# Two attentions of a Flamingo layer pair: heads written out without a loop, new orders of TensorE's work within a step, and identity matmuls

## The chip, the core and the metric

The kernel runs on one core of a Trainium2 chip. The metric is the device time in microseconds (us) of one execution; before the change the median of three runs is 1977.64 us (1966.12 to 1983.28). The core has five engines that run beside each other and meet at semaphores: TensorE (matmuls; PE in the profile, its weight loads PEld), VectorE (DVE), ScalarE (ACT), GpSimd (POOL) and SyncE (SP), which here issues transfers.

## The reference

Two layers, each a gated cross-attention and a gated mixture of experts, over 2048 tokens of width 256 and 1601 context rows:

```python
x = x + jnp.tanh(g_xattn[0]) * _L0_xattn_ref(_layernorm(x), ctx, ctx, mask, ...)
x = x + jnp.tanh(g_ffn[0])   * _L0_ffn_ref(_layernorm(x), ...)
x = x + jnp.tanh(g_xattn[1]) * _L1_xattn_ref(_layernorm(x), ctx, ...)
x = x + jnp.tanh(g_ffn[1])   * _L1_ffn_ref(_layernorm(x), ...)
```

Both attentions have 16 heads of depth 16:

```python
q, k, v = _proj(query, wq, bq), _proj(ctx, wk, bk), _proj(ctx, wv, bv)
scores = jnp.einsum('bhqd,bhkd->bhqk', q, k) / 4
scores = jnp.where(mask == 0, -jnp.inf, scores)     # layer 0 only
x = jnp.einsum('bhqk,bhkd->bhqd', jax.nn.softmax(scores, axis=-1), v)
return jnp.einsum('bsd,ed->bse', x, wo) + bo
```

In layer 0 the mask leaves nearly all keys out: the mask is zero for the keys that are valid. The kernel finds the keys that count at run time, and where they fit into a window of 512 keys it attends to that window alone. They do for these inputs. Layer 1 attends to all 1601 keys.

## The kernel before

`flamingo_kernel` runs stages one after the other: projections of the context, normalisation and queries, `attend_masked` (layer 0), output projection, experts, and the same for layer 1 with `attend`. The change touches `attend` (L589 on) alone, which both attentions use, with a `Keys` object for the sizes: the windowed one has KT = 4 key tiles of 128 and one maxima piece of 512 keys for each query tile; the full one has KT = 13 and four pieces of 399 to 402 keys. A third branch, all keys with the mask, isn't taken.

For each head three kinds of work are done, and three heads are in flight at once. **Maxima**: queries times keys with the queries as weights, in pieces of a PSUM bank, of which VectorE takes the row maxima (L793, L900); 64 pieces a head in the full attention, 16 in the windowed one. TensorE then turns the finished maxima (L782), VectorE splits them into two parts (L906, L908), and SP sends these as two more rows of the queries (L726). **Scores**: keys times queries, with the maxima subtracted by those rows, in four chunks of 512 queries for each key tile (L804); ScalarE takes the exponential of each (L883). **Values**: probabilities times values for the four chunks of a key tile, in four column groups of the array, accumulated in one bank over the head (L821); column 16 of the values is one and so gives the sums. ScalarE copies the bank out (L866), TensorE turns it with four transposes (L786, "sums"), VectorE divides (L916, L919).

Queries and keys lie twice in SBUF, once on partitions 0 to 50 and once on 64 to 114; 48 to 51 rows are contracted, so a matmul takes one half of the array's rows. Score chunks 0 and 2 use the lower half, 1 and 3 the upper; maxima pieces take turns (`tile_of`, piece number modulo 2). Scores have three banks (`s_bank`), pieces, turned maxima and sums share four (`p_bank`), values have one.

An iteration `i` has KT steps. It makes the maxima of head i, all but the last LATE key tiles' scores of head i-1 (from step LATE on), and the last LATE key tiles of head i-2 (steps 0 to LATE-1); values follow one step behind their scores. LATE is 4 in the full and 2 in the windowed attention. `entries` lists the pieces of each step (four or five; four in the windowed one), with "maxima" put in at step 1 (windowed: step 0) behind two pieces, and "sums" last in step 6 (windowed: 3). `body` of the tensor block (L826 on) writes out the order of a step by hand: chunks 0 and 1, two pieces, chunk 2, one piece, values, chunk 3, the rest. Waits: a score waits until the exponential three chunks before has freed its bank; a piece waits until VectorE has done the piece four places before; the first score of a head waits for the two rows with its maxima; a head's first values wait until the bank has been copied out. ScalarE's copy stands in step LATE before chunk 3's exponential.

`iterations` (L681 on) gives the order of heads to each engine: iterations 0 to 3 written out, 4 to 15 as a loop of four passes over three iterations, 16 and 17 written out. SP has a loop of its own of the same form.

## Time and profile before

| | us |
|---|---|
| three runs | 1966.12, 1977.64, 1983.28 |
| the profiled execution | 1979.84 |
| its span, first to last instruction | 1978.0 |
| TensorE busy | 1660.8 (84%) |
| VectorE busy | 1051.4 (53%) |
| ScalarE busy | 767.8 (39%) |
| maxima pieces on VectorE (L900), 1280 | 672.6 |
| exponentials on ScalarE (L883), 1088 | 565.5 |
| maxima matmuls on TensorE (L793), 1280 | 425.8 |
| score matmuls on TensorE (L804), 1088 | 410.5 |
| values matmuls on TensorE (L821), 2176 records | 325.4 |
| mean granted clock of TensorE | 0.873 |

The busy times of an engine's lines are unions and can overlap with each other. The two attentions lie at about 169 to 408 us (windowed) and 995 to 1670 us (full) of the span.
### The profile page before, as it was taken

The page shows a single profiled execution, that of the slowest core. Times are in us where ns is not written, and L with a number is a line of the kernel's source. Part 1 is how long each engine was busy: PE and PEld are TensorE (multiplying, and loading weights), DVE is VectorE, ACT ScalarE, POOL GpSimd, SP SyncE. Part 2 cuts the span into 40 slices and gives each one's busy share as a digit, 9 for nine tenths or more (in the row PEclk, how much of TensorE's full clock was granted, in tenths as well). Part 3 has the DMA queues.
Part 4 walks back from the last instruction along what each step waited for, and adds up shares of the span by engine and source line. Part 5 has one row for each costly group of instructions (what it writes and reads, how often), then busy time and mean ns, then how long its engine had stood idle before and what let it go on. Part 6 is the DMA issues. An engine that isn't in the chain of part 4 may idle for free. (4 is left out here: it accounts for less than half of the span.)

```text
span 1978.0 us, 26775 instructions
## 1 busy us (share of the span) xinstructions
PE 1660.8 (84%) x7489; PEld 864.0 (44%) x7490; DVE 1051.4 (53%) x2222; ACT 767.8 (39%) x1486; POOL 174.5 (9%) x243
## 2 busy tenths in 40 slices
PE   6465999969998999994499999999999999786880
PEld 3132444345665566662254444444444433543550
DVE  2565688652211122224398888787887841522334
ACT  3031577621111121120317776676776774121110
POOL 3610000000300000003000000000000000051106
PEclk9785699978999999997759998898998995697995
DMA  7934221111100987882632121111211100424114
GB/s 245 365 139 130 56 49 49 26 44 64 43 0 22 328 304 286 305 304 80 181 86 64 41 42 22 24 22 24 42 22 23 23 2 0 106 77 130 40 45 130
DMA packets 108696, 197.16 MB, mean 100 GB/s; under 512 B 8958, under 2 KB 80371, under 8 KB 108567
## 3 DMA queue, kind: packets, MB, share of 16 engines
q1 hardware_dynamic: 101633, 180.71, 29.3%
q0 software_dynamic: 4608, 12.59, 2.0%
q10 hardware_dynamic: 2326, 2.31, 0.4%
q8 instruction: 61, 1.00, 0.2%
q14 instruction: 68, 0.56, 0.1%
HBM read 144.69 MB, written 50.36 MB: 99 GB/s over the span
## 5 line engine op out<-in xcount | busy, mean ns | idle before, releaser
L900 DVE TENSOR_REDUCE attend_piece_max<-attend_p_bank 128x1 f32<-128x400 f32 (+3 forms) x1280 | 672.6, 590 | 155.3 <-PE attend_p_bank L793 147.5
L883 ACT ACTIVATE attend_probs<-attend_s_bank 128x512 f32<-128x512 f32 (+1 forms) x1088 | 565.5, 601 | 333.4 <-PE attend_s_bank L804 332.8
L793 PE MATMUL attend_p_bank<-attend_k_st,attend_q_st 48*128 48x400 f32 (+2 forms) x1280 | 425.8, 432 | 47.0 <-DMA attend_k_st<-ones_rows 21.1
L804 PE MATMUL attend_s_bank<-attend_q_st,attend_k_st 50*128 50x512 f32 (+2 forms) x1088 | 410.5, 493 | 32.7 <-ACT attend_probs L883 11.8
L804 PEld LDWEIGHTS attend_s_bank<-attend_q_st,attend_k_st 50*128 50x128 f32 (+2 forms) x1088 | 182.2, 198 | 385.5 <-ACT attend_probs L883 307.3
L821 PE MATMUL attend_o_bank<-attend_probs,attend_v_st 128*32 128x512 f32 (+1 forms) x2176 | 325.4, 673 | 1.4 <-ACT attend_probs L883 1.4
L793 PEld LDWEIGHTS attend_p_bank<-attend_k_st,attend_q_st 48*128 48x128 f32 (+1 forms) x1280 | 231.7, 207 | 92.4 <-issue 43.9
L1498 DVE TENSOR_TENSOR slots_hid<-slots_b_bank,slots_g_act 128x512 f32<-128x512 f32 x46 | 31.8, 692 | 159.9 <-PE slots_b_bank L1392 159.9
L1279 DVE TENSOR_TENSOR share_hid<-share_b_bank,share_g_act 128x512 f32<-128x512 f32 (+1 forms) x40 | 27.6, 691 | 149.1 <-PE share_b_bank L1160 149.1
L1468 ACT ACTIVATE slots_g_act<-slots_a_bank 128x512 f32<-128x512 f32 x46 | 27.5, 597 | 169.4 <-PE slots_a_bank L1392 169.4
L1392 PE MATMUL slots_a_bank<-slots_w_up,slots_x_t 128*128 128x512 f32 x184 | 88.1, 602 | 5.4 <-DMA slots_w_up<-in_L_ffn_W_dram 5.4
L1392 PE MATMUL slots_b_bank<-slots_w_up,slots_x_t 128*128 128x512 f32 x184 | 86.5, 592 | 0.0
L1414 PE MATMUL slots_y_bank<-slots_w_dn,slots_hid_t 128*128 128x256 f32 x368 | 83.3, 379 | 1.0 <-DVE slots_hid_t L1455 1.0
L1707 POOL DMA_INDIRECT collect_back<-back,keep_f_place x48 | 46.7, 974 | 422.6 <-PEq L1696 408.6
L1414 PEld LDWEIGHTS slots_y_bank<-slots_w_dn,slots_hid_t 128*128 128x128 f32 x368 | 69.8, 190 | 20.0 <-issue 11.7
L1160 PE MATMUL share_a_bank<-keep_x_x_nt,share_w_up 128*128 128x512 f32 (+1 forms) x160 | 78.6, 615 | 0.0
L1610 PE MATMUL slots_u_bank<-keep_f_up,slots_x_t 128*128 x156 | 63.6, 532 | 17.8 <-issue 15.9
L821 PEld LDWEIGHTS attend_o_bank<-attend_probs,attend_v_st 128*32 128x32 f32 (+1 forms) x2176 | 44.5, 112 | 76.9 <-ACT attend_probs L883 57.0
L1131 POOL DMA_INDIRECT sorted<-keep_x_x_n,keep_f_place x48 | 46.4, 966 | 349.3 <-DVE keep_f_place L1264 335.3
L768 POOL COPY attend_v_st<-attend_values 128x64 f32 (+3 forms) x32 | 9.3, 298 | 768.7 <-PE attend_o_bank L821 737.0
L1160 PE MATMUL share_b_bank<-keep_x_x_nt,share_w_up 128*128 128x512 f32 (+1 forms) x160 | 76.3, 600 | 0.0
L1171 PE MATMUL share_y_bank<-share_w_dn,share_hid 128*128 128x256 f32 (+1 forms) x320 | 71.2, 382 | 5.9 <-DVE share_hid L1279 5.9
(208 smaller groups left out, 1368.2 us busy)
## 6 DMA issues: line engine op xcount, KB each, us to landing
slots_w_up<-in_L_ffn_W_dram SPq DMA_DIRECT2D x46, 1024.0 KB, 6.9
slots_w_dn<-in_L_ffn_W_dram SPq DMA_DIRECT2D x23, 1024.0 KB, 6.7
ctx_raw<-in_mask_BxSxS_ik_dram SPq DMA_DIRECT2D x16, 800.5 KB, 8.3
q_rows<-q_part SPq DMA_DIRECT2D x24, 512.0 KB, 4.0
attend_q_st<-q_rows SPq DMA_DIRECT2D x64, 192.0 KB, 4.5
k_rows<-ctx_k_part SPq DMA_DIRECT2D x12, 800.5 KB, 10.5
attend_k_st<-k_rows SPq DMA_DIRECT2D x32, 300.2 KB, 5.9
sorted<-keep_zeros SPq DMA_DIRECT2D x6, 1024.0 KB, 6.7
```

The source lines that it names most:

```text
L793: last = pe.matmul(bank[:, 0:even(kn)], q_st[rows, slot, t * P:(t + 1) * P].bitcast(F32R), k_st[rows, slot, k0:k0 + even(kn)].bitcast(F32R ...
L804: last = pe.matmul(out, k_st[rows, hs, kt * P:kt * P + kn].bitcast(F32R), q_st[rows, hs, q0:q0 + CH].bitcast(F32R), start=True, stop=not m ...
L821: last = pe.matmul(o_bank[c * VW:(c + 1) * VW, :], v_st[0:kn, hs, kt, :], probs[0:kn, (kt + hs) % RING, c * CH:(c + 1) * CH], start=(kt == ...
L883: act.activation(probs[0:kn, (kt + hs) % RING, q0:q0 + CH], s_bank[(NC * kt + c + hs) % RING][0:kn, :], ACT.Exp).then_inc(exp_done, 1)
L900: dve.tensor_reduce(dst, bank_of(i, n)[:, 0:kn], AX.X, ALU.max).then_inc(entry_done, 1)
L1131: pool.indirect_dma_start(scratch["sorted"][l][:, :], bass.IndirectOffsetOnAxis(ap=place[:, k, t:t + 1], axis=0), x_n[:, t], None).then_in ...
L1160: last = pe.matmul(bank[n % 2][0:FW, :], w_up[:, which, b, f * FW:(f + 1) * FW], x_nt[:, b, c * CH:(c + 1) * CH], start=(b == 0), stop=(b ...
L1171: last = pe.matmul(y_bank[n % 2][:, :], hid[:, c % 2, f, t * P:(t + 1) * P], w_dn[:, f], start=(f == 0), stop=(f == FT - 1))
L1392: last = pe.matmul(bank[k][:, 0:HW], x_t[:, slot, b], w_up[:, slot, which, b, half * HW:(half + 1) * HW], start=(b == 0), stop=(b == DB - 1))
L1414: last = pe.matmul(y_bank[:, 0:D], hid_t[:, slot, f], w_dn[:, slot, f], start=(f == 0), stop=(f == FT - 1))
L1610: last = pe.matmul(u_bank[k][:, 0:2 * F], x_t[:, k, b], resident["up"][:, e, b].rearrange("p a n f -> p (a n f)"), start=(b == 0), stop=(b ...
L1707: pool.indirect_dma_start(back[:, k, t], None, scratch["back"][l][:, :], bass.IndirectOffsetOnAxis(ap=place[:, k, t:t + 1], axis=0))\
```

## The change

`Keys` gets a flag `looped`; only the branch that isn't taken sets it, so for both attentions that run, every engine's iterations and SP's are written out. In `body` of the tensor block a step has one of two orders, by the half of its first piece (EVEN: lower, also where a step has no pieces; ODD: upper), and values come after all scores and pieces, followed by the sums. `keep_busy` multiplies a bf16 identity by itself, four times repeated to 512 columns, into the bank that the next entry will overwrite: twice ahead of the turned maxima and of the sums, twice ahead of each piece in steps 0 and 1 of the windowed attention's iteration 1, and twelve times in iteration 16 ahead of the wait for the last head's maxima. ScalarE's copy of the values' bank moves from step LATE before chunk 3 to step LATE+1 before chunk 2.

```diff
--- before.py
+++ after.py
@@ -380,7 +380,8 @@
 class Keys:
 
 
-    def __init__(self, first, size, pieces, late, maxima_at):
+    def __init__(self, first, size, pieces, late, maxima_at, looped=False):
+        self.looped = looped
         self.first, self.S, self.pieces = first, size, pieces
         self.KT = -(-size // P)
         self.late = late
@@ -637,6 +638,11 @@
         ENTRIES = PER + 4
         assert ENTRIES % BANKS == 0 and (NC * KT) % RING == 1
 
+        EVEN = [("entry", slice(0, 2)), ("score", 0), ("score", 1), ("entry", slice(2, 4)), ("score", 2), ("score", 3),
+                ("entry", slice(4, None))]
+        ODD = [("entry", slice(0, 1)), ("score", 0), ("score", 1), ("entry", slice(1, 2)), ("entry", slice(2, 3)),
+               ("score", 2), ("entry", slice(3, 4)), ("score", 3), ("entry", slice(4, None))]
+
         def entries(mx, tail, fresh):
 
 
@@ -682,11 +688,12 @@
 
             def once(i):
                 body(i, i % RING, i < H, i >= 2, 1 <= i <= H)
-            for i in range(4):
+            for i in range(4 if keys.looped else H):
                 once(i)
-            with eng.Fori(4, H - RING + 1, RING) as j:
-                for u in range(RING):
-                    body(j + u, (4 + u) % RING, True, True, True)
+            if keys.looped:
+                with eng.Fori(4, H - RING + 1, RING) as j:
+                    for u in range(RING):
+                        body(j + u, (4 + u) % RING, True, True, True)
             for i in range(H, H + 2):
                 once(i)
 
@@ -744,10 +751,11 @@
                 for t, n in clears[2 * i - 2:2 * i]:
                     sp.dma_start(scratch["sorted"][l][t * P:(t + n) * P, :].rearrange("(t p) d -> p t d", p=P),
                                  const["zeros"][:, :].unsqueeze(1).to_broadcast([P, n, D])).then_inc(cleared, 16)
-            with sp.Fori(4, H - RING, RING) as j:
-                for u in range(RING):
-                    body(j + u, (4 + u) % RING, True, True, True)
-            for i in range(H - RING, H + 1):
+            if keys.looped:
+                with sp.Fori(4, H - RING, RING) as j:
+                    for u in range(RING):
+                        body(j + u, (4 + u) % RING, True, True, True)
+            for i in range(H - RING if keys.looped else 4, H + 1):
                 body(i, i % RING, True, True, True)
             sp.wait_ge(cleared, 16 * len(clears))
 
@@ -774,9 +782,16 @@
             pe.wait_ge(fixed, 2 + (SP > S))
             pe.wait_ge(rows_in, 16 * (6 if row_masked else 2))
 
-            def entry(i, slot, what, n):
+            def keep_busy(bank, times):
+
+                for _ in range(times):
+                    pe.matmul(bank[:, :], const["ident_bf"][:, :],
+                              const["ident_bf"][:, :].unsqueeze(1).to_broadcast([P, CH // P, P]), start=True, stop=True)
+
+            def entry(i, slot, what, n, extra=0):
                 wait(pe, entry_done, entries_before(i) + (n - BANKS + 1))
                 bank = bank_of(i, n)
+                keep_busy(bank, extra if extra else 2 * isinstance(what, str))
                 if what == "maxima":
                     wait(pe, max_ready, i)
                     last = pe.transpose(bank[0:QT, 0:P], row_max[:, (slot - 1) % RING, :], const["ident"][:, :])
@@ -833,14 +848,24 @@
                 for s in range(KT):
                     now, before = score_step(i, slot, s, tail, fresh), pv_step(i, slot, s, tail, fresh)
                     if now and now[2] == 0:
+                        if isinstance(i, int) and i == H:
+                            pe.wait_ge(entry_done, entries_before(i) + places("maxima"))
+                            keep_busy(p_bank[0], 12)
                         wait(pe, max_in, i * (16 * PART))
-                    for chunks, first, end in (((0, 1), 0, 2), ((2,), 2, 3), ((3,), 3, None)):
-                        if chunks == (3,) and before:
-                            times_values(*before)
-                        for c in chunks if now else ():
-                            scores(*now, c)
-                        for what, at in listed[s][first:end]:
-                            entry(i, slot, what, at)
+                    raising = row_masked and isinstance(i, int) and i == 1 and s < LATE
+                    pieces = [x for x in listed[s] if x[0] != "sums"]
+                    sides = [what % 2 for what, _ in pieces if not isinstance(what, str)]
+                    order = ODD if sides and sides[0] else EVEN
+                    for kind, at in order:
+                        if kind == "score" and now:
+                            scores(*now, at)
+                        elif kind == "entry":
+                            for what, n in pieces[at]:
+                                entry(i, slot, what, n, 2 * raising)
+                    if before:
+                        times_values(*before)
+                    for what, n in listed[s][len(pieces):]:
+                        entry(i, slot, what, n)
 
             iterations(pe, body)
 
@@ -868,7 +893,7 @@
             def body(i, slot, mx, tail, fresh):
                 for s in range(KT):
                     now = score_step(i, slot, s, tail, fresh)
-                    if not now and s == LATE and tail:
+                    if not now and s == LATE + 1 and tail:
                         copy_out(i)
                     if now:
                         h, hs, kt = now
@@ -876,7 +901,7 @@
                         if not isinstance(h, int) or KT * h + kt >= RING:
                             wait(act, pv_done, h * KT + (kt - 2))
                         for c in range(NC):
-                            if c == NC - 1 and s == LATE and tail:
+                            if c == 2 and s == LATE + 1 and tail:
                                 copy_out(i)
                             q0 = chunk_of(c)
                             wait(act, score_ready, h * (NC * KT) + (NC * kt + c + 1))
@@ -1765,7 +1790,8 @@
         }
         x_now, stats = sc.sb("x_now", [P, QT, D], F32), sc.sb("stats", [P, QT, 6], F32)
         make_constants(nc, io, const, scratch)
-        everything = Keys(0, S, PIECES, 4, (1, 2))
+        everything = Keys(0, S, PIECES, 4, (1, 2), looped=True)
+        unmasked = Keys(0, S, PIECES, 4, (1, 2))
         for l in range(2):
             if l:
                 clear_semaphores(nc)
@@ -1788,7 +1814,7 @@
                 if l == 0:
                     attend_masked(nc, const, scratch, everything, attn, row_max, mask_all, window)
                 else:
-                    attend(nc, const, scratch, l, everything, attn, row_max)
+                    attend(nc, const, scratch, l, unmasked, attn, row_max)
                 project_out(nc, const, l, attn, row_max, io["x"][0] if l == 0 else None, x_now, stats)
             with ExitStack() as part:
                 keep = Scope(nc, part, f"keep_f{l}")
```

## Rows read from the trace of the kernel before

**Rows 1.** Windows, the two attentions: busy us (instructions) of each engine, clock, DMA

```profile
177.60:242.70 65.10, 63.89 (x243) 27.38 (x243) 44.23 (x82) 31.53 (x61) 0.71 (x3) 0.58 0.30 84
242.70:380.70 138.00, 131.47 (x756) 55.50 (x756) 122.54 (x232) 97.39 (x188) 2.37 (x10) 1.00 0.18 44
1168.00:1211.70 43.70, 42.69 (x226) 18.56 (x225) 33.50 (x70) 27.44 (x54) 0.36 (x1) 0.80 0.13 25
1211.70:1249.00 37.30, 35.04 (x220) 15.10 (x219) 33.25 (x69) 26.83 (x52) 0.36 (x1) 1.00 0.17 29
1249.00:1292.80 43.80, 40.45 (x231) 18.22 (x231) 33.39 (x69) 28.11 (x55) 0.36 (x1) 0.88 0.14 26
1367.50:1412.20 44.70, 41.87 (x231) 18.91 (x231) 33.42 (x70) 28.27 (x55) 0.36 (x1) 0.85 0.13 25
1486.90:1533.60 46.70, 43.34 (x231) 19.62 (x231) 33.42 (x70) 28.27 (x55) 0.36 (x1) 0.82 0.13 24
```

**Rows 2.** Timeline at a pass of the loop: start, length, instructions, idle before

```profile
1251.12 0.91 PE L804 MATMUL attend_s_bank<-attend_q_st,attend_k_st 50*128 50x512 f32 x2 [3.08 <-issue]
```

**Rows 3.** Waits, full attention: who waited for whom, us in total, times, longest

```profile
PEld attend_s_bank L804 <- ACT attend_probs L883: 239.0, 366, 1.7
```

**Rows 4.** Timeline of TensorE, two regular steps of the full attention

```profile
1156.49 0.49 PE L804 MATMUL attend_s_bank<-attend_q_st,attend_k_st 50*128 50x512 f32 x1
1156.83 0.34 PE L793 MATMUL attend_p_bank<-attend_k_st,attend_q_st 48*128 48x400 f32 x1
1157.10 1.06 PE L821 MATMUL attend_o_bank<-attend_probs,attend_v_st 128*32 128x512 f32 x8
1158.09 0.49 PE L804 MATMUL attend_s_bank<-attend_q_st,attend_k_st 50*128 50x512 f32 x1
...
1158.39 0.39 PE L804 MATMUL attend_s_bank<-attend_q_st,attend_k_st 50*128 50x512 f32 x1
...
1158.61 0.39 PE L804 MATMUL attend_s_bank<-attend_q_st,attend_k_st 50*128 50x512 f32 x1
1158.62 0.56 PE L793 MATMUL attend_p_bank<-attend_k_st,attend_q_st 48*128 48x400 f32 x2
1159.28 0.50 PE L804 MATMUL attend_s_bank<-attend_q_st,attend_k_st 50*128 50x512 f32 x1
1159.43 0.44 PE L793 MATMUL attend_p_bank<-attend_k_st,attend_q_st 48*128 48x400 f32 x1
1159.81 0.64 PE L821 MATMUL attend_o_bank<-attend_probs,attend_v_st 128*32 128x512 f32 x4
```

**Rows 5.** Timeline of TensorE, steps without maxima pieces, tail of the full attention

```profile
1626.07 0.49 PE L804 MATMUL attend_s_bank<-attend_q_st,attend_k_st 50*128 50x512 f32 x1 [0.45 <-ACT attend_probs L883]
1626.49 1.06 PE L821 MATMUL attend_o_bank<-attend_probs,attend_v_st 128*32 128x512 f32 x8
...
1629.13 1.93 PE L821 MATMUL attend_o_bank<-attend_probs,attend_v_st 128*32 128x512 f32 x8
...
1633.20 1.08 PE L821 MATMUL attend_o_bank<-attend_probs,attend_v_st 128*32 128x512 f32 x4
```

**Rows 6.** Page, costliest groups: the exponentials, busy us, mean ns, idle before

```profile
L883 ACT ACTIVATE attend_probs<-attend_s_bank 128x512 f32<-128x512 f32 (+1 forms) x1088 | 565.5, 601 | 333.4 <-PE attend_s_bank L804 332.8
```

**Rows 7.** Page, costliest groups: 512-column f32 matmuls over the full array

```profile
L1392 PE MATMUL slots_a_bank<-slots_w_up,slots_x_t 128*128 128x512 f32 x184 | 88.1, 602 | 5.4 <-DMA slots_w_up<-in_L_ffn_W_dram 5.4
```

**Rows 8.** Timeline of TensorE, full head, around the sums

```profile
1228.76 1.06 PE L821 MATMUL attend_o_bank<-attend_probs,attend_v_st 128*32 128x512 f32 x8
...
1230.36 0.66 PE L786 MATMUL attend_p_bank<-keep_ident,attend_o_sb 128*128 128x128 f32 x4
1230.95 0.50 PE L804 MATMUL attend_s_bank<-attend_q_st,attend_k_st 50*128 50x512 f32 x2
...
1232.23 0.44 PE L793 MATMUL attend_p_bank<-attend_k_st,attend_q_st 48*128 48x400 f32 x1 [0.22 <-DVE keep_a_attn L919]
1232.60 0.64 PE L821 MATMUL attend_o_bank<-attend_probs,attend_v_st 128*32 128x512 f32 x4
```

## The prediction

> **What bounds the kernel now.** I read the stages first, by windows over each head of the two attentions, then the granted clock in them, then what TensorE waits for, then TensorE's own timeline. The first attention is the windowed one (four key tiles), the second the full one (thirteen). A full head at the upper clock (2.4 GHz, granted 1.00) takes 37.3 us [rows 1]: thirteen steps, in which TensorE is busy 35.0 us, VectorE 33.3 and ScalarE 26.8. Neither VectorE nor ScalarE is full. Three heads, the first of each later pass of the loop, take 43.8, 44.7 and 46.7 us [rows 1], and there TensorE stands still 3.08 us for "issue", with nothing that it waits for, before its first score chunk [rows 2]; then the granted clock falls to 0.50 (1.2 GHz) for part of the head, which makes the mean 0.82 to 0.88. One head, 1168.0 to 1211.7, is as slow (43.7 us, clock 0.80) with no such gap. The other cold places are the windowed attention's first heads (177.6 to 242.7, clock 0.58) and the tails, where only scores and values are left: there a step is 2.64 us long (1626.49 to 1629.13) and then, at the lower clock, 4.07 [rows 5].
>
> Inside a step at the upper clock the longest wait is the weight load of a score chunk for the exponential that frees its bank: 239.0 us in the full attention [rows 3]. The timeline shows the ring [rows 4]. With the values starting at 1157.10, the next work starts at 1158.09 (+0.99): score chunk 3. The next score starts at 1158.39 (+1.29), behind a piece in its half. Chunk 2 of the next key tile starts at 1159.28, 1.19 after chunk 3, since its bank is freed by chunk 3's exponential (three banks, four chunks). A piece follows, and the values start at 1159.81. So 0.99 + 1.19 + 0.53 = 2.71 us per step; where the piece after chunk 2 shares its half (1156.49, 1156.83, 1157.10) the last term is 0.61 and the step 2.79; with no piece it is 0.42 (1626.07 to 1626.49) [rows 5]. Mean of both kinds 2.75. That ring, not the columns that TensorE streams, sets the step.
>
> **The change, part by part.**
>
> *No loop.* The three gaps and the cold stretches behind them cost 43.8 + 44.7 + 46.7 - 3 x 37.3 = 23.3 us, and the same instructions in a straight line leave no such gap in the heads before the loop. I take -23. Bounds: -9 (the gaps alone, 3 x 3.1, if the clock falls anyway) to -30 (the unprovoked fall, 6.4 us, goes too). The windowed attention's eleven heads from 242.7 to 380.7 take 12.5 us each with clock 1.00 [rows 1], so its loop costs nothing that can be won. SP's and POOL's bodies are unrolled too; their loads stay behind the same waits, a head ahead.
>
> *The orders in a regular step.* The ring keeps its form: values, first score, its exponential, the score three chunks later, values. It is now chunk 0 that comes first and chunk 3 that waits for it. In an even step (first piece in half 0) two pieces stand ahead, chunk 0 is second in its half: its start moves from +0.99 to +1.29, but a score that starts first has its weight load in front (0.49 against 0.39 long), so its result is late by 0.30 - 0.10 = 0.20 [rows 4]. Chunk 3 then starts at 2.38, the fifth piece is in the other half: 2.38 + 0.53 = 2.91. In an odd step the one piece ahead is in the other half, chunk 0 starts at +0.99, the fifth piece shares chunk 3's half: 2.18 + 0.61 = 2.79. Step 0 has four pieces: 2.38 + 0.42 = 2.80. So the new orders do not shorten a regular step; they lengthen even ones by 0.1 to 0.2. The pieces add nothing: VectorE is busy 33.3 of 37.3 us [rows 1], a step's five pieces take it some 2.5 us of these 2.8 to 2.9, and its four banks carry it over the values' 0.99; if it were late, the wait of the fifth piece for the bank of the first would be next.
>
> *Copy out of the values' bank.* It moves one step on and behind two exponentials. The next values wait for it: first exponential at about 1.73, two at 0.52 (565.5 us over 1088), the copy, of the same shape, 0.60 [rows 6]: values at 3.3 instead of 2.91, against about 2.95 in the old order (chunk 2 held by 0.2): +0.35. Formerly it went ahead of chunk 3's exponential and held chunk 2 a little. Queued behind it on ScalarE are chunks 2 and 3, ready in time.
>
> *Identity matmuls.* Two ahead of each transpose of the maxima and of the sums, 512 columns of bf16, full array. No row has one. Bounds: 0 if they fall wholly in a wait, 0.47 each from 512-column f32 records (88.1 us over 184) [rows 7]. I take 0.23, the distance at which the next work in the same half follows a 512-column score (1158.39 to 1158.62; nearest in columns and in being one record) [rows 4]. Sums: formerly the first transpose starts at 1230.36 and scores resume at 1230.95, values at 1232.60, 3.84 after those of 1228.76 [rows 8], because the third maxima piece (1232.23) waits until the sums are normalised, 1.87 after the first transpose; some 0.4 of these VectorE spends on a piece queued before. Now: values 0, identities 1.0, transposes 1.65, resumed at 2.2, chunk 0 at 2.5, chunk 3 at 3.55, the fifth piece needs VectorE (sums normalised at 3.15, first piece done at 3.7): values at 4.1. Maxima: formerly they came last before the values, where only the values' own change of mode followed. Now they stand between chunk 1 and the third piece: two more changes between half and full array; the last piece waits for the split maxima, about 3.15: values at 3.5.
>
> Full head: 2.80 + 3.5 + 6 x 2.79 + 3 x 2.91 + 3.3 + 4.1 = 39.2 against 37.3: +1.9, times 14 heads: **+26**. Bounds: -57 if every step shrank to VectorE's 33.3 us per head; +40 with identities at 0.47.
>
> *Windowed head.* Four even steps of four pieces. The two regular ones tie (chunk 0 later by 0.2, but no piece between chunk 3 and the values, 0.42 against 0.61). The copy costs +0.4; sums and maxima now follow each other with four identities and the second waits for the normalised sums: +1.1. +1.5 x 14 = **+21**. Bounds: 0 and +34.
>
> *Raising the clock.* In iteration 1 of the windowed attention two identities stand ahead of each of eight pieces (16 at twice 0.23 while cold, 7 us, partly over the wait for the first maxima). From 177.6 to 242.7 four iterations take 65.1 us [rows 1]; at 12.5 us each, with some 2.5 for identities that nothing covers, they would take 52.5. So -13 if the clock rises there and stays. Bounds: +4 (it doesn't rise) to -15.
>
> *Twelve at the end*, before head 15's first score in both attentions: 12 x 0.23 + 0.1 = 2.9 us each on the path, as nothing is queued that could hide them. A tail step costs 1.43 more at 1.2 GHz [rows 5]. If they hold the clock for four more steps in the windowed tail and three in the full one, they return 10: -4 net. Bounds: +6 to -15.
>
> **Sum**: -23 + 26 + 21 - 13 - 4 = +7 on the profiled execution's 1979.8 us, which lies 2.2 over the median 1977.6: **1984 us**.
>
> **A rule weighed.** In the rows a weight load is hidden even in the same half: the piece at 1158.62 follows its score by 0.23 us, no more than 512 columns' stream at 2.4 GHz. The Trainium skill (TensorE: Matmul & The Clock Gate, Part 3, "What overlaps and what doesn't") says that a weight load overlaps a running matmul only when the row group differs. By that rule opposite halves side by side would save a load on one or two neighbours a step. The trace disagrees wherever the load is not behind a semaphore; behind one it shows 0.61 against 0.53, a gain of 0.08. A second one speaks against the change: TensorEngine Tiling (Array Packing), "Key Properties", has a change of tiling mode drain the array; the added switches at the maxima would be dearer than I take them.
>
> **Rivals.**
> 1. *The orders cost nothing* (27%). If the identities and the copy lie in waits that the ring has anyway (239 us of them), the 26 and 21 vanish: 1984 - 47 = 1937. For it: TensorE waits about 1.1 us a step for ScalarE. Against: those waits lie ahead of the third-next score, and the additions stand ahead of the first.
> 2. *Same-half neighbours were the price* (6%): behind a wait, a piece starts 0.34 after a score of its own half and 0.15 after one of the other (1156.83, 1159.43) [rows 4]; 0.19 saved in each of 208 + 64 steps is 52 us: 1984 - 52 = 1932. The skill's rule above would give this.
> 3. *The clock falls more often* (20%), the other side. Regular steps stretch, so TensorE does less per us; the head from 1168.0, slow without a gap, shows how near the level is [rows 1]. Place: the copy and sums steps of full heads. Each fall costs 6.4. Three more, and no rise in the windowed attention (+17): 1984 + 19 + 17 = 2020. It decides from two further falls (1997).
> 4. *The identities do hold the clock* (4%): no unprovoked fall, windowed and full tails warm: 1984 - 6 - 20 = 1958.
> 5. My forecast, 43%, own range 1962 to 2006; of it 6% lies above +1%.
>
> A change under 1% (20 us) is what a measurement of this kernel cannot tell from none: its three runs span 17 us. Faster by over 1%: 27 + 6 + 4 = 37%. Slower: 20 + 6 = 26%. Within: 37%. The range takes rivals 1 and 2 in with room for partly hidden terms (1925) and stops between my upper bound and rival 3 (2012).
>
> **What would show it.** No "issue" gap of 3 us at heads 7, 10 and 13; full heads of 39 us where the clock is 1.00 (rival 1: 37.3; rival 2: below 35); first score at +1.29 in even steps and +0.99 in odd ones, values to values 2.9 and 2.8; about 4.1 after the sums. Windowed heads of 14 us; clock 1.00 from about 190 us. Wrong it would be, above all, if chunk 3 didn't wait for chunk 0's exponential, or if the cold stretches stay though the gaps go.

## The result and the profile after

The changed kernel takes 2033.16 us (median of four, 2029.45 to 2037.07) against 1977.18: the ratio is 1.029, 95% interval 1.0239 to 1.0341. It is slower by 2.9%, above the range. A ratio here and below compares only those executions of a kernel whose clock was little disturbed, and so can say more or less than the medians. The page of the profiled execution (2029.45 us); PEclk is the granted clock in 40 slices, in tenths:

```profile
span 2027.7 us, 23161 instructions
...
PE 1680.6 (83%) x7657; PEld 848.2 (42%) x7658; DVE 1052.9 (52%) x2222; ACT 767.0 (38%) x1486; POOL 173.6 (9%) x243
...
PEclk9785999988999999996669899898999995797995
```

TensorE is busy longer, at about the same mean clock, and the tenths drop to 8 again and again over the full attention. Windows over the two attentions (busy us and instructions of PE, PEld, DVE, ACT, POOL; clock; DMA) answer to [rows 1]; the last row is the full attention's tail:

```profile
178.60:241.10 62.50, 57.64 (x273) 21.23 (x273) 44.67 (x83) 31.05 (x60) 0.71 (x3) 0.83 0.31 88
241.10:395.60 154.50, 136.16 (x801) 52.86 (x801) 122.69 (x231) 97.30 (x187) 2.38 (x10) 1.00 0.16 40
1155.00:1197.20 42.20, 38.75 (x231) 15.96 (x231) 33.27 (x69) 27.44 (x53) 0.36 (x1) 0.92 0.14 25
1240.30:1279.60 39.30, 35.93 (x231) 14.95 (x233) 33.28 (x70) 27.43 (x53) 0.36 (x1) 1.00 0.16 27
1651.30:1719.70 68.40, 61.28 (x234) 16.76 (x235) 1.46 (x5) 35.70 (x70) 0.00 (x0) 0.65 0.00 1
```

The windowed attention's eleven later heads take 154.5 / 11 = 14.05 us each, formerly 12.5. A full head at the upper clock takes 39.3 us, formerly 37.3, with VectorE busy the same 33.3. But such heads are rare: of the fifteen intervals between the ends of heads' maxima in the full attention, nine are 42 to 43 us like the one from 1155.0, clock 0.92, and one is 40.5. A head's maxima count as ended when VectorE begins to join them. Summed over the profiles, from the first head's maxima to the last's, the full attention went from 590.9 to 619.9 us (+29.0), the windowed one from 203.1 to 217.0 (+13.9), the tails behind them from 24.6 to 25.0 and from 58.5 to 68.4 (+10.3); the rest gives 3.5 back; the span's difference is 49.7.

Two regular steps answer to [rows 4]:

```profile
1187.54 1.07 PE L836 MATMUL attend_o_bank<-attend_probs,attend_v_st 128*32 128x512 f32 x8
1188.54 0.44 PE L808 MATMUL attend_p_bank<-attend_k_st,attend_q_st 48*128 48x402 f32 x1
1188.54 0.67 PE L819 MATMUL attend_s_bank<-attend_q_st,attend_k_st 50*128 50x512 f32 x2
...
1189.78 0.50 PE L819 MATMUL attend_s_bank<-attend_q_st,attend_k_st 50*128 50x512 f32 x1
1190.12 0.34 PE L808 MATMUL attend_p_bank<-attend_k_st,attend_q_st 48*128 48x400 f32 x1
1190.39 1.07 PE L836 MATMUL attend_o_bank<-attend_probs,attend_v_st 128*32 128x512 f32 x8
1191.39 0.45 PE L808 MATMUL attend_p_bank<-attend_k_st,attend_q_st 48*128 48x400 f32 x2
1191.68 0.40 PE L819 MATMUL attend_s_bank<-attend_q_st,attend_k_st 50*128 50x512 f32 x2
...
1192.82 0.49 PE L819 MATMUL attend_s_bank<-attend_q_st,attend_k_st 50*128 50x512 f32 x1 [0.32 <-ACT attend_probs L908]
...
1193.24 0.64 PE L836 MATMUL attend_o_bank<-attend_probs,attend_v_st 128*32 128x512 f32 x4
```

The ring has the form that was foretold. In the odd step a piece and the first score start together at 1188.54 (+1.00), chunk 3 at 1189.78 (+2.24), then a piece of its own half, and the values at 1190.39: 2.85 in all. In the even step two pieces start (1191.39), the scores follow behind them (+1.29), chunk 3 starts at 1192.82 (+2.43) together with its piece, and the values at 1193.24: again 2.85. The waits, which answer to [rows 3], have moved from scores behind exponentials to pieces behind VectorE, without anything gained. The first row is the kernel before, beside the 239.0 us of [rows 3]; the other two are the changed kernel:

```profile
PEld attend_p_bank L793 <- DVE attend_piece_max L900: 13.9, 54, 0.5
PEld attend_p_bank L808 <- DVE attend_piece_max L925: 126.6, 171, 1.7
PEld attend_s_bank L819 <- ACT attend_probs L908: 101.8, 176, 1.1
```

The step with the copy of the values' bank, TensorE's rows and then ScalarE's:

```profile
1168.97 1.07 PE L836 MATMUL attend_o_bank<-attend_probs,attend_v_st 65*32 65x512 f32 x8
...
1171.39 0.50 PE L819 MATMUL attend_s_bank<-attend_q_st,attend_k_st 50*128 50x512 f32 x1 [0.33 <-ACT attend_probs L908]
...
1172.41 1.59 PE L836 MATMUL attend_o_bank<-attend_probs,attend_v_st 128*32 128x512 f32 x8 [0.53 <-issue]
1173.93 0.70 PE L808 MATMUL attend_p_bank<-attend_k_st,attend_q_st 48*128 48x400 f32 x1
```

```profile
1170.74 1.09 ACT L908 ACTIVATE attend_probs<-attend_s_bank 128x512 f32<-128x512 f32 x2 [0.97 <-PE attend_s_bank L819]
1171.71 0.60 ACT L891 ACTIVATE attend_o_sb<-attend_o_bank 128x512 f32<-128x512 f32 x1
1172.19 1.10 ACT L908 ACTIVATE attend_probs<-attend_s_bank 128x512 f32<-128x512 f32 x2
```

The last score starts at 1171.39, its piece with it; the values could follow at 1171.8 (estimated from the 0.42 us between them in the even step). But the copy (L891) starts only at 1171.71, behind two exponentials, and TensorE stands, that is, has nothing to do, for 0.53 us; the step is 1172.41 - 1168.97 = 3.44 us. What follows at 1173.93 starts 1.52 behind the values instead of 1.0: the granted clock falls to 0.50 at 1172.8. In each of the ten slow heads the clock falls in this step: copies that start at 1086.4, 1128.4, 1171.7, 1213.7, 1296.1, 1339.1, 1381.1, 1463.5, 1506.5 and 1625.8 us, and falls recorded at 1087.5, 1128.5, 1172.8, 1213.8, 1295.7, 1340.1, 1381.0, 1463.0, 1507.3 and 1626.8. In the kernel before, the two falls that no loop's return explains lay at the same place, 1.2 and 1.9 us behind the start of a copy (falls at 1181.8 and 1509.5).

The stand isn't always ahead of the fall, though. Five of the ten falls are recorded 0.9 to 1.1 us behind the start of the copy, two as it starts, and three (1295.7, 1381.0, 1463.0) before it. At the last of these the score ahead of the stand is already long, 0.79 us instead of 0.50:

```profile
1463.15 0.79 PE L819 MATMUL attend_s_bank<-attend_q_st,attend_k_st 50*128 50x512 f32 x1 [0.33 <-ACT attend_probs L908]
...
1464.18 1.94 PE L836 MATMUL attend_o_bank<-attend_probs,attend_v_st 128*32 128x512 f32 x8 [0.23 <-issue]
```

So the stand of the same step can't have brought down the clock in these three; that stands are the cause at all has to be shown by taking them away.

### The profile page after: what moved, and what is told of

It reads as the page before. It is cut to its first block and busy times, and to the rows that moved or that the text cites. A ratio compares the mean times of both kernels' runs of the same rounds, so it can differ in the third digit from the quotient of the medians.

```text
span 2027.7 us, 23161 instructions
## 1 busy us (share of the span) xinstructions
PE 1680.6 (83%) x7657; PEld 848.2 (42%) x7658; DVE 1052.9 (52%) x2222; ACT 767.0 (38%) x1486; POOL 173.6 (9%) x243
## 5 line engine op out<-in xcount | busy, mean ns | idle before, releaser
L808 PE MATMUL attend_p_bank<-attend_k_st,attend_q_st 48*128 48x400 f32 (+2 forms) x1280 | 388.6, 445 | 46.5 <-DMA attend_k_st<-ones_rows 20.9
L819 PE MATMUL attend_s_bank<-attend_q_st,attend_k_st 50*128 50x512 f32 (+2 forms) x1088 | 374.9, 461 | 57.4 <-ACT attend_probs L908 49.4
L836 PE MATMUL attend_o_bank<-attend_probs,attend_v_st 128*32 128x512 f32 (+1 forms) x2176 | 319.5, 662 | 15.1 <-issue 15.1
L808 PEld LDWEIGHTS attend_p_bank<-attend_k_st,attend_q_st 48*128 48x128 f32 (+1 forms) x1280 | 196.6, 203 | 302.1 <-DVE attend_piece_max L925 178.7
L819 PEld LDWEIGHTS attend_s_bank<-attend_q_st,attend_k_st 50*128 50x128 f32 (+2 forms) x1088 | 166.1, 196 | 184.7 <-ACT attend_probs L908 162.5
L941 DVE RECIPROCAL attend_inv_sum<-attend_p_bank 128x16 f32<-128x16 f32 x32 | 8.2, 257 | 143.3 <-PE attend_p_bank L801 143.3
L776 POOL COPY attend_v_st<-attend_values 128x64 f32<-128x64 f32 (+1 forms) x32 | 9.4, 300 | 804.9 <-PE attend_o_bank L836 774.5
```

What stands on the lines that cost most here:

```text
L808: last = pe.matmul(bank[:, 0:even(kn)], q_st[rows, slot, t * P:(t + 1) * P].bitcast(F32R), k_st[rows, slot, k0:k0 + even(kn)].bitcast(F32R ...
L819: last = pe.matmul(out, k_st[rows, hs, kt * P:kt * P + kn].bitcast(F32R), q_st[rows, hs, q0:q0 + CH].bitcast(F32R), start=True, stop=not m ...
L836: last = pe.matmul(o_bank[c * VW:(c + 1) * VW, :], v_st[0:kn, hs, kt, :], probs[0:kn, (kt + hs) % RING, c * CH:(c + 1) * CH], start=(kt == ...
```

## The experiments

All were timed beside the kernel before. Medians of that kernel moved between 1970 and 1979 us from one group to the next. Names that begin with a stand for edits of the changed kernel, those with b for edits of the kernel before. "Copy step" is the time from values to values, in the full attention and at 2.4 GHz, in the step in which ScalarE copies the values' bank out. "Falls" counts falls of the clock between the first and the last head's maxima of the full attention in one execution, the profiled one, and such counts differ between executions: the profiled one of `b_noloop_late` was the fastest of its four, those of `a_nobusy` and `b_noloop_later` the slowest and second slowest.

| kernel | median us | ratio (95%) | copy step | full, windowed head at 2.4 GHz | falls |
|---|---|---|---|---|---|
| before | 1970 to 1979 | 1 | 2.97 | 37.3, 12.5 | 5 |
| after | 2033 | 1.029 (1.024 to 1.034) | 3.45 | 39.3, 14.0 | 10 |
| b_noloop | 1941.6 | 0.980 (0.972 to 0.988) | 2.88 | 37.1, 12.3 | 2 |
| b_noloop_late | 1937.5 | 0.989 (0.977 to 1.001) | 3.20 | 37.5, 12.6 | 0 |
| b_noloop_later | 2007.7 | 1.010 (1.000 to 1.020) | 3.70 | 37.9, 13.1 | 7 |
| b_noloop_raise | 1936.7 | 0.987 (0.978 to 0.997) | 2.88 | 37.1, 12.3 | 3 |
| b_sooner | 1925.2 | 0.976 (0.971 to 0.981) | 2.78 | 37.7, 11.8 | 1 |
| b_sooner_raise | 1926.2 | 0.976 (0.971 to 0.981) | 2.78 | 37.7, 11.8 | 0 |
| b_mixed | 1936.6 | 0.977 (0.969 to 0.986) | 2.89 | 37.1, 11.8 | 3 |
| b_one | 1955.4 | 0.991 (0.987 to 0.995) | 2.80 | 38.3, 11.8 | 5 |
| a_looped | 2074.6 | 1.047 (1.039 to 1.055) | 3.39 | 38.8, 14.0 | 11 |
| a_nobusy | 2026.4 | 1.021 (1.013 to 1.029) | 3.45 | 38.9, 13.7 | 12 |
| a_no12 | 2023.8 | 1.026 (1.016 to 1.036) | 3.45 | 39.3, 14.0 | 10 |
| a_copy | 1976.7 | 1.009 (1.006 to 1.012) | 2.80 | 38.6, 13.4 | 2 |
| a_copy_nobusy | 1976.5 | 1.001 (0.996 to 1.006) | 2.80 | 38.2, 13.0 | 5 |
| a_copy_first | 1963.4 | 0.997 (0.992 to 1.001) | 2.75 | 38.2, 12.8 | 4 |
| a_late_first | 1986.4 | 1.008 (1.002 to 1.013) | 3.26 | 38.7, 13.3 | 7 |

**The loop.** `b_noloop` writes out the loops of the kernel before, with nothing else (the hunks of the change with `looped` in them). `a_looped` puts them back into the changed kernel:

```diff
-        unmasked = Keys(0, S, PIECES, 4, (1, 2))
+        unmasked = Keys(0, S, PIECES, 4, (1, 2), looped=True)
```

and the same flag for the windowed keys.

> The kernel before with only its loops written out; orders, copy and identities as before. Theory A (the loop's gaps pull the clock down, and the changed kernel lost that gain by its later copy out of the values' bank): full heads of 37.3 us, no issue gap of 3 us, at most two clock falls between heads 2 and 15, time 1977 - 23 = 1954 (1945 to 1962). Theory B (without the loop the clock falls at head boundaries anyway, since the gaps were not the cause): cold heads every second or third one, time 1970 to 1985. Theory C (straight-line code is fetched more slowly): steps longer than 2.71 and 2.79 at the upper clock, over 1985.

> The changed kernel with its loops kept (orders, copy and identities stay). Theory A: the three gaps of 3 us come back at heads 7, 10 and 13 with cold stretches beside the falls at the copy: 2033 + 9 to + 20 = 2042 to 2053. Theory B (the clock falls anyway): only the gaps themselves return, 2042. If writing the loop out gained nothing at all: 2033.

Writing the loops out is worth 37 us by the medians before the change (1941.6) and 41 after it (2074.6 against 2033.2), more than the 23 that I took; the ratios say 39 and 35. `a_looped` came out slower than any of its three expectations. Two falls were left in `b_noloop`; the first of them cost 10 us. In its profile 19 us were gained in the full attention, 3 in the windowed one (heads of 12.3 instead of 12.5 us, so that loop cost something too) and 16 in the tails, whose iterations were written out before as well; these 16 are a later fall of the clock, and no run shows that the loop has a part in them.

**The copy.** `a_copy` takes the copy ahead of chunk 0's exponential in the same step of the changed kernel:

```diff
-                            if c == 2 and s == LATE + 1 and tail:
+                            if c == 0 and s == LATE + 1 and tail:
```

> The changed kernel with ScalarE's copy of the values' bank ahead of chunk 0's exponential in the same step instead of chunk 2's. Theory A: the values no longer stand 0.5 us for the copy, step 5 is 2.9 to 3.0 instead of 3.45, full heads 38.8, windowed 13.5, and the falls at the copy go (at most three in the full attention instead of nine): 2033 - 8 - 8 - 25 = 1992. Theory B or D: the steps shorten the same way but the falls stay: 2015 to 2020.

It measures 1976.7, faster than the 1992 of theory A: by the medians one line gives back the whole of the change's 56 us, by the ratios (1.029 to 1.009) some 40. Its copy step and a stretch of nine heads without a fall:

```profile
1187.37 1.06 PE L836 MATMUL attend_o_bank<-attend_probs,attend_v_st 65*32 65x512 f32 x8
...
1189.74 0.50 PE L819 MATMUL attend_s_bank<-attend_q_st,attend_k_st 50*128 50x512 f32 x1 [0.26 <-ACT attend_probs L908]
...
1190.16 0.64 PE L836 MATMUL attend_o_bank<-attend_probs,attend_v_st 128*32 128x512 f32 x4
```

```profile
1041.60:1383.00 341.40, 316.77 (x2022) 131.31 (x2021) 294.09 (x610) 243.37 (x471) 3.25 (x9) 1.00 0.18 36
```

There is no stand ahead of the values at 1190.16. Of the 56 us, 20 are 0.7 us in each full and 0.65 in each windowed head, 25 are falls in the full attention (its time over 15 heads at the upper clock went from 30.4 to 5.2 us), and 8 lie in the full tail. This doesn't hang on the one profile: worked out from span and mean granted clock (twice the missing share, times the span), the four executions of the changed kernel spent 483 to 507 us each at 1.2 GHz, the ten of `a_copy` 370 to 420. `b_noloop_late` and `b_noloop_later` bring the stand to the old orders, written out and without identities:

```diff
-                            if c == NC - 1 and s == LATE and tail:
+                            if c == 1 and s == LATE + 1 and tail:
```

with `c == 2` in the second, and in both the line for steps without scores one step on, as in the change.

> The kernel before, written out, with ScalarE's copy of the values' bank moved one step on and ahead of chunk 1's exponential, so that the next values wait for it by some 0.4 us; old orders, no identities. Theory A: full heads 37.2 + 0.3 = 37.5 and windowed 12.3 + 0.3, and falls of the clock at the copy in most heads (+3 to 4 each, 14 heads): 1942 + 10 + 40 = 1990. If only the late copy together with the new orders does it: 1952, with three falls or fewer.

> The kernel before, written out, with the copy one step on and ahead of chunk 2's exponential: in the old order the values then stand about 0.9 us for it instead of 0.4. Theory A1: with a stand twice that of the changed kernel the clock falls at every copy, 1940 + 7 + 7 + 45 = 1999. Theory A2: the other steps of the head stay at 2.75, at most three or four falls, 1940 + 14 + 5 = 1959.

With the copy behind one exponential TensorE stands 0.34 us in each head, and in the profiled execution the clock stays at 1.00 from 1022.8 to 1579.2 us, nearly the whole attention:

```profile
1202.31 1.06 PE L824 MATMUL attend_o_bank<-attend_probs,attend_v_st 65*32 65x512 f32 x8
...
1204.83 0.34 PE L796 MATMUL attend_p_bank<-attend_k_st,attend_q_st 48*128 48x400 f32 x1
1205.52 1.07 PE L824 MATMUL attend_o_bank<-attend_probs,attend_v_st 128*32 128x512 f32 x8 [0.34 <-issue]
```

```profile
1022.80:1579.20 556.40, 531.24 (x3327) 231.26 (x3327) 482.94 (x1001) 408.52 (x790) 4.71 (x13) 1.00 0.16 30
```

Behind two it stands 0.84 us, and the clock falls at about every second copy, in six of seven falls for 17 us:

```profile
1157.36 1.06 PE L824 MATMUL attend_o_bank<-attend_probs,attend_v_st 65*32 65x512 f32 x8
...
1161.06 0.64 PE L824 MATMUL attend_o_bank<-attend_probs,attend_v_st 128*32 128x512 f32 x4 [0.84 <-issue]
```

```profile
1134.50:1199.40 64.90, 61.20 (x386) 26.74 (x388) 57.86 (x120) 47.93 (x93) 0.72 (x2) 1.00 0.17 30
1199.40:1216.40 17.00, 17.00 (x70) 7.84 (x62) 8.87 (x19) 6.97 (x15) 0.00 (x0) 0.50 0.07 11
1216.40:1281.30 64.90, 61.24 (x386) 26.79 (x388) 57.86 (x120) 47.81 (x93) 0.72 (x2) 1.00 0.16 30
```

Over all executions `b_noloop_later` spent 490 to 576 us at 1.2 GHz and `b_noloop` 409 to 464; `b_noloop_late`, with 361 to 461, isn't set apart from `b_noloop`. My theory as first written (any such stand) fell with the first of the two; and A2, by which the stretched steps around the stand are needed, fell with the second, whose regular steps are the old 2.71 and 2.79. `a_late_first` (the changed kernel, late copy, chunk 0 first as below) was to part these two:

> The changed kernel (late copy, identities, written out) with chunk 0 ahead of the first two pieces in even steps, so that only the regular steps get shorter (2.85 to 2.72) while the values still stand for the copy. Theory A1 (the stand of the values itself pulls the clock down): still eight or nine falls at the copy, 2033 - 6 - 9 = 2018. Theory A2 (the stand does it only where the steps around it are stretched too, since TensorE then does too little in the whole stretch): three falls or fewer, 2033 - 15 - 25 = 1993.

It lies between: seven falls, but all of one head in two at the copy, and most cost only 1.2 us instead of 3 to 4. So neither order nor stand settles it alone: with the copy step at 3.20 us there was no fall, with 3.26, 3.39, 3.45 and 3.70 there were seven to twelve, in old and new orders, and what each cost depended on the order around it. Nor is a stand needed for every fall: the five of `a_copy_nobusy` and three of the five of `b_one` come 1 to 2 us behind copies that nothing waits for. The clock is apt to fall at this place in all kernels; with the long stand it falls there often. How the stand does that stays open.

**The identities.** `a_nobusy` and `a_copy_nobusy` have none; `a_no12` lacks the twelve of iteration 16; `b_noloop_raise` adds only those of the windowed attention's iteration 1, meant to raise the clock there ("raising" below), to the written-out kernel before.

```diff
-                keep_busy(bank, extra if extra else 2 * isinstance(what, str))
+                keep_busy(bank, extra)
...
-                    raising = row_masked and isinstance(i, int) and i == 1 and s < LATE
+                    raising = False
...
-                            keep_busy(p_bank[0], 12)
```

> The changed kernel without any identity matmul; orders, copy and written-out heads stay. Theory A (late copy holds the values 0.5 us and the clock falls there): the falls stay, one head in two, at the copy; full heads at the upper clock 39.3 - 0.9 = 38.4; windowed heads 14.05 - 0.9 = 13.1, their first ones cold again (+7); time 2033 - 13 - 13 + 7 - 6 = 2008. Theory B (the identities are what tips the clock, by the drains around them): no falls inside the full attention, 1980. Theory D (the identities hold the clock as far as it is held): falls at every head, over 2040.

> The changed kernel with the early copy and without any identity matmul. If the late copy alone pulls the clock down (theory A), no more than three falls in the full attention and full heads at 38.6 - 0.5 = 38.1, windowed 13.0, first windowed heads cold (+7): 1977 - 8 - 6 + 7 = 1970. If the identities also hold the clock (theory D), falls at the sums of most heads (+3 to 4 us each): 2000 or more.

> The changed kernel without the twelve identities ahead of the last head's scores. If they only cost: the step of 5.35 us in the full tail becomes 2.66 and that of the windowed tail loses as much: 2033 - 6 = 2027. If they hold the clock in the tails (returning 10 as the forecast had it): 2033 + 4 = 2037, with cold stretches that begin earlier in both tails.

> The kernel before, written out, with the identities in the windowed attention's iteration 1 alone (two ahead of each of eight pieces and of the maxima). If they raise the clock there: 1.00 from about 200 us, iterations 1 to 4 take 18 + 3 x 12.4 + 2 = 57 us instead of 65, time 1942 - 8 = 1934. If the clock rises no earlier than 233: 1942 + 4 = 1946.

Those at the head boundaries cost 0.4 us a head, where 0.92 are streamed: the step of the sums takes 3.82 us with them and 3.43 without, the step of the maxima 3.54 either way. With them less time was spent at 1.2 GHz (370 to 420 against 411 to 488 us, ten executions each, early copy; in the profiles 10 us of the difference lie ahead of the rise in the windowed attention). The sum is nil (1976.5 against 1976.7). The twelve cost what they take, 2.76 us here:

```profile
1661.36 1.06 PE L836 MATMUL attend_o_bank<-attend_probs,attend_v_st 128*32 128x512 f32 x8
1662.36 2.76 PE L788 MATMUL attend_p_bank<-keep_ident_bf 128*128 128x512 bf16 x12
1665.06 0.73 PE L819 MATMUL attend_s_bank<-attend_q_st,attend_k_st 50*128 50x512 f32 x3
...
1666.72 0.64 PE L836 MATMUL attend_o_bank<-attend_probs,attend_v_st 65*32 65x512 f32 x4
```

They return nothing in the full tail, where the clock fell at 1671.2 all the same; without them the median is 9 us lower, within what the intervals leave open. The raising identities make iteration 1 14.7 to 20.2 us long (18.5 in the changed kernel) instead of 10.3 to 12.5. The clock rose at 183 to 202 us in the eight profiles with them and at 187, 188, 190, 190, 199, 211, 223, 233 and 233 us in the nine without. So they replace a wide spread by a narrower one, at a price of four to eight us; `b_noloop_raise` is no faster than `b_noloop` beyond their intervals, nor `b_sooner_raise` than `b_sooner`.

**The orders.** `a_copy_first` is `a_copy` with chunk 0 ahead of the pieces in even steps (the line's first half):

```diff
-        EVEN = [("entry", slice(0, 2)), ("score", 0), ("score", 1),
+        EVEN = [("score", 0), ("entry", slice(0, 2)), ("score", 1),
```

> The changed kernel with the early copy, and in even steps chunk 0 ahead of the first two pieces. Ring theory (the first score after the values, its exponential, the score three later): even steps go from 2.85 to 2.7 (0.99 + 1.19 + 0.53), odd ones stay at 2.8; full heads 38.6 - 7 x 0.14 = 37.7, windowed 13.4 - 4 x 0.17 = 12.7, time 1977 - 13 - 10 = 1954. If the pieces in front cost nothing (VectorE or the streams set the step): 1977.

```profile
1198.31 1.06 PE L836 MATMUL attend_o_bank<-attend_probs,attend_v_st 128*32 128x512 f32 x8
1199.30 0.49 PE L819 MATMUL attend_s_bank<-attend_q_st,attend_k_st 50*128 50x512 f32 x1
...
1200.54 0.50 PE L819 MATMUL attend_s_bank<-attend_q_st,attend_k_st 50*128 50x512 f32 x1 [0.15 <-ACT attend_probs L908]
...
1201.02 0.64 PE L836 MATMUL attend_o_bank<-attend_probs,attend_v_st 128*32 128x512 f32 x4
```

Chunk 0 starts at +0.99, chunk 3 at +2.23, values at +2.71. Full heads went from 38.6 to 38.2, windowed from 13.4 to 12.8, time from 1976.7 to 1963.4. The ring holds; in full heads the gain was smaller than foretold (0.4 against 0.9 us), above all because the step of the maxima took 3.77 us instead of 3.53.

`a_copy_nobusy` against `b_noloop` shows what the orders do: neither has a loop or an identity, and beside the orders only the place of the copy differs, for which the values stand in neither. It is 1976.5 against 1941.6 us, so 35 us, some 26 of them in heads at the upper clock (38.2 and 37.1 in the full, 13.0 and 12.3 in the windowed attention). Half of a full head's 1.1 us is in the step of the maxima and the one behind it: together 5.87 us before, 6.40 with the values behind all pieces (in the changed kernel the last piece waits some 0.4 us until VectorE has split the maxima).

`b_sooner` leaves the change's idea and acts on the ring's last term: values right behind the score that waits.

```diff
-                    for chunks, first, end in (((0, 1), 0, 2), ((2,), 2, 3), ((3,), 3, None)):
+                    for chunks, first, end in (((0, 1), 0, 2), ((2,), 2, 2), ((3,), 2, None)):
```

`b_sooner_raise` adds the raising identities; `b_mixed` uses this order in the windowed attention alone; `b_one` has one piece instead of two ahead of chunk 2 in the full one.

> The kernel before, written out, with the values right behind chunk 2, and all pieces but the first two behind chunk 3. Ring theory: no piece is left between the score that waits and the values, so a regular step is 0.99 + 1.19 + 0.42 = 2.60 instead of 2.71 and 2.79: full heads 37.2 - 13 x 0.15 = 35.2, windowed 12.3 - 4 x 0.2 = 11.5, time 1940 - 29 - 11 = 1900. If VectorE is the limit by then (33.3 busy, pieces bunched behind the values): 36.5 and 1925. If the order of pieces is indifferent: 1940.

> The same with two identities ahead of each piece of the windowed attention's iteration 1. Clock 1.00 from about 200 us instead of about 233: 8 us less than without, 1892; where the clock rises by itself at 190, as in one profile of the kernel with the late copy and no identities, no gain or a loss of 5.

> The kernel before, written out, with the values right behind chunk 2 in the windowed attention alone and the old order in the full one. Windowed heads 11.8 instead of 12.3 (8 us), full heads 37.2 as in the old order instead of 37.7 (8 us less than b_sooner): 1941 - 8 = 1933 if the old order's two or three falls of the clock stay, 1917 if they go.

> As b_mixed, and in the full attention one piece instead of two ahead of chunk 2, none between it and the values, four behind chunk 3. If only the piece that waits for VectorE (at +2.35 in b_sooner) held chunk 2 up: steps of 2.60, full heads 36.0, time 1925 - 27 = 1898. If VectorE's rate is the limit in the bunch of four: 37.5 to 38 and 1925 to 1930.

Windowed heads fall to 11.8 us (11.5 expected). In full heads the second theory won, but with 37.7 us for the 36.5 that it named:

```profile
1204.57 1.07 PE L824 MATMUL attend_o_bank<-attend_probs,attend_v_st 128*32 128x512 f32 x8
...
1206.92 0.45 PE L796 MATMUL attend_p_bank<-attend_k_st,attend_q_st 48*128 48x400 f32 x1 [0.24 <-DVE attend_piece_max L903]
1206.92 0.50 PE L807 MATMUL attend_s_bank<-attend_q_st,attend_k_st 50*128 50x512 f32 x1
1207.35 0.64 PE L824 MATMUL attend_o_bank<-attend_probs,attend_v_st 128*32 128x512 f32 x4
```

The piece ahead of chunk 2 waits for VectorE until 1206.92 (+2.35), and chunk 2 with it, which could have started at +2.18: 2.78 a step, 37.7 a head. With one piece ahead (`b_one`) it is no better (38.3, at 1955 us, where 1925 to 1930 was the dearest expected): VectorE, busy 33.3 us a head, gets four in a bunch. `b_mixed`, with the old order's 37.1 us in full heads, measures 1936.6 for the 1933 expected with falls. So full heads are slower in `b_sooner` than in the old order (37.1), and its gain over `b_noloop` lies in the windowed heads and in the clock. At 1925 us it is the fastest measured, 2.4% under the kernel before; `b_mixed`, `b_noloop` and `b_sooner_raise` lie within its interval.

## Why the prediction was wrong

- **Right: the ring and what it makes of the orders.** Full head 39.2 forecast, 39.3 measured; windowed head 14.0 and 14.05; even steps 2.91 and 2.85, odd 2.79 and 2.85; after the maxima 3.5 and 3.54; identities 0.23 each. The +26 and +21 were +30 (15 heads at 2.0) and +22. That 39.2 is so near is in part luck: the copy step came out 0.15 longer, the one after the sums 0.28 shorter (3.82 for 4.1), and in the even step a later chunk 3 (2.43 for 2.38) met a shorter last term (0.42 for 0.53).
- **Wrong: "Copy out of the values' bank ... +0.35".** The stand was found and priced as time alone, and the sum held the clock where it was. It is the line on which the result hangs: 40 to 56 us by `a_copy`, of which 20 are the stand (0.7 a head; 3.45 where 3.3 was forecast and 2.8 without it) and the rest mostly the clock. So the -23 was won at the loop and lost again at the copy: beyond 15 heads at the upper clock the full attention spent 31.4 us before (590.9 - 15 x 37.3) and 30.4 after (619.9 - 15 x 39.3). By stages, the forecast had +3 for the full attention (-23 + 26) and it is +29; +8 for the windowed one (21 - 13) and it is +14; -4 for the tails and it is +10. Rival 3 had the place right, "the copy and sums steps", but three more falls at 6.4 us each where there are ten at 3 on average, and 20% where the trace had already shown a fall 1.2 us behind a copy.
- **Wrong in size: "I take -23".** Bounded at -30, it is -37 and -41 by the medians. The excess makes the kernel faster and so can't explain the miss; in the profile of `b_noloop` the full attention, for which it was worked out, gave 19. "Its loop costs nothing that can be won" missed 0.2 us a windowed head.
- **Wrong: "So -13 if the clock rises there and stays".** Iterations 1 to 4 went from 65.1 to 62.5 us [rows 1]. The clock did rise at 200 us, but iteration 1 grew by 6 us, and the late rise at 233 that was to be saved is one draw of a spread of 187 to 233.
- **Wrong in sign: "-4 net" for the twelve.** They cost 2.8 and held nothing in the full tail, which grew by 9.9 us, mostly by the clock.
- Rivals 1 and 2 fell. The orders cost 35 us and the copy 40 to 56, so the waits of the ring hid neither; of the identities alone they hid half (0.4 us a head shown, 0.92 streamed). Opposite halves shortened no step: both kinds grew, from 2.71 and 2.79 to 2.85.

## What to carry to other kernels

Where a ring of few buffers sets the step, place only the work that the ring needs between its links; here a piece less ahead of the first or behind the waiting score was worth 0.1 to 0.2 us a step where VectorE kept up, and nothing where it didn't (full heads of `b_sooner`); pairing halves was worth nothing. Price a stand of TensorE twice, as time and by what the clock does around it, and look in the trace for where the clock last fell without a gap. Count falls over several executions, not in one. Where a loop's return leaves TensorE idle in the trace, write the loop out first and alone.

## What the runs showed of the hardware

Returning to the start of a long loop body leaves TensorE idle 2.6 to 4.0 us in the full attention (thirteen steps, three heads; six returns, in the kernel before and in `a_looped`). In the windowed one (four steps, three heads) there is no such gap, but its heads take 12.5 us looped and 12.3 written out. A stand of TensorE of 0.34 us once in 37.5 us left the granted clock at 1.00 for 556 us in one execution; with one of 0.53 in 39.3, TensorE busy 35.9 of the 39.3 us, it fell at two copies in three, and with one of 0.84 in 37.9, busy 61.2 of 64.9, at one in two. Mean busy shares do not order these: `a_copy`, 316.8 of 341.4 us, has a lower one than `b_noloop_later` and hardly any fall. What brings the clock down stays open. So does why it rises at different times in kernels whose code there is much alike. Executions of one kernel lie 8 (the changed kernel, `b_sooner`) to 59 us (the kernel before, 14 executions) apart.
